# Attention stage of a fused block: transposes moved to a slot's end, projections and scores ahead of the first values

## The reference

```
x = x + 0.5 * ffn(layernorm(x))      # mixture of experts and a shared expert
x = x + attention(layernorm(x))
x = x + 0.5 * ffn(layernorm(x))

attention(X):                        # 16 query heads, 8 key/value heads, head size 32
    q, k, v = X @ Wq, X @ Wk, X @ Wv
    q, k = rope(q), rope(k)
    att = 50 * tanh(q @ k.T / 16 / 50)         # soft cap
    y = softmax(where(causal, att, -inf)) @ v
    return y @ Wo
```

## Time and profile before

| | |
|---|---|
| median of 3 runs | 1038.65 us (1037.8 to 1040.78) |
| the profiled execution | 1037.34 us, its span 1034.9 us |
| PE matmul busy | 943.6 us, 91% of the span |
| DVE, ACT, POOL busy | 631.3, 500.4, 463.0 us |
| mean granted TensorE clock | 0.981 of full |
| scores of the first slot start | 364.64 us |
| scores of the last slot start | 678.76 us |

### The profile page before, as it was taken

How to read it: one execution, slowest core, us unless ns; L and a number is a source line. 1 busy time by engine, 2 the same in 40 slices (tenths; PEclk the granted TensorE clock), 3 DMA queues, 4 the chain that set the end, 5 groups by cost and what they waited for, 6 DMA issues and landing times. The chain is left out here.

```text
span 1034.9 us, 17824 instructions
## 1 busy us (share of the span) xinstructions
PE 943.6 (91%) x6146; PEld 698.0 (67%) x6146; DVE 631.3 (61%) x1669; ACT 500.4 (48%) x733; POOL 463.0 (45%) x502
## 2 busy tenths in 40 slices
PE   2999998999999479999999999986999989999998
PEld 1788876777778446565556655544888867777787
DVE  4888777444445445656565656635888777453435
ACT  3766732132234057675667666653766532232322
POOL 5333204565541164666456645633422223655530
PEclk9999999999999699999999999998999999999999
DMA  5433235777764300000100010012243255777735
GB/s 185 117 107 113 74 102 148 173 182 179 178 152 101 123 1 21 21 20 21 41 20 21 20 41 21 12 61 75 64 130 110 69 162 124 181 184 178 177 65 167
DMA packets 95430, 101.88 MB, mean 98 GB/s; under 512 B 18688, under 2 KB 86656, under 8 KB 95360
## 3 DMA queue, kind: packets, MB, share of 16 engines
q1 hardware_dynamic: 83072, 83.17, 27.1%
q0 software_dynamic: 12288, 17.83, 10.2%
HBM read 65.44 MB, written 35.54 MB: 98 GB/s over the span
## 5 line engine op out<-in xcount | busy, mean ns | idle before, releaser
L80 PE MATMUL gu<-x_hi,gu_hi 128*128 128x512 f32 x308 | 139.1, 452 | 4.8 <-DVE act_gu L1124 4.8
L1585 POOL TENSOR_SCALAR_AFFINE_SELECT probs_at<-probs_at 128x1024 f32<-128x1024 f32 x64 | 71.1, 1111 | 133.7 <-ACT probs_at L1528 133.7
L82 PE MATMUL gu<-x_lo,gu_hi 128*128 128x512 f32 x308 | 121.9, 396 | 0.0
L81 PE MATMUL gu<-x_hi,gu_lo 128*128 128x512 f32 x308 | 121.3, 394 | 0.0
L1520 ACT ACTIVATE capped_at<-scores_at 128x2048 f32<-128x2048 f32 x64 | 93.2, 1456 | 36.8 <-PE scores_at L1434 36.8
L671 POOL DMA_INDIRECT rows<-z_rows,slots x64 | 68.8, 1075 | 75.4 <-DVE slots L1115 56.4
L957 ACT CAST a_hi<-act_gu 128x512 fp32r<-128x512 f32 x96 | 59.2, 616 | 83.8 <-DVE act_gu L1124 64.0
L1528 ACT ACTIVATE probs_at<-capped_at 128x2048 f32<-128x2048 f32 x64 | 95.0, 1485 | 2.0
L80 PE MATMUL down<-down_hi,a_hi 128*128 128x256 f32 x300 | 93.7, 312 | 0.2 <-DVE a_lo L1134 0.2
L867 PE MATMUL zT<-w_gu,xT 128*128 128x352 f32 x256 | 86.3, 460 | 0.0
L81 PE MATMUL down<-down_hi,a_lo 128*128 128x256 f32 x300 | 83.7, 279 | 0.0
(11 more groups left out here) (218 smaller groups left out, 2394.7 us busy)
## 6 DMA issues: line engine op xcount, KB each, us to landing
w_gu<-in_w_gate SPq DMA_DIRECT2D x64, 176.0 KB
w_gu<-in_w_up SPq DMA_DIRECT2D x64, 176.0 KB
w_down<-in_w_down SPq DMA_DIRECT2D x64, 176.0 KB
z_rows<-z SPq DMA_DIRECT2D x16, 512.0 KB, 3.1
acc<-base SPq DMA_DIRECT2D x10, 512.0 KB, 3.6
out<-base SPq DMA_DIRECT2D x10, 512.0 KB, 3.7
x_f<-in_X SPq DMA_DIRECT2D x8, 512.0 KB, 4.7
xn_at<-acc SPq DMA_DIRECT2D x16, 256.0 KB, 2.7
```

Of the source, the lines that this page charges most:

```text
L80: nc.tensor.matmul(out, w_hi, x_hi, start=first, stop=False)
L81: nc.tensor.matmul(out, w_lo, x_hi, start=False, stop=False)
L82: return nc.tensor.matmul(out, w_hi, x_lo, start=False, stop=last)
L1585: pool.affine_select(out=diag, in_=diag, compare_op=ALU.is_ge, fill=zero, base=0, pattern=[[0, JH], [0, REP], [1, P]], channel_multiplier= ...
```

## The change

Nothing is added or removed; instructions of the attention slots change places on PE, ACT, POOL and DVE. SP's queue is the same.

```diff
@@ TensorE
-            def slot_of(b, q, behind=True, ahead=True):
+            def slot_of(b, q, behind=True, ahead=True, further=True):
                 score_unit(b, q, 0)
-                if ahead:
-                    transposes(b + 1)
                 if behind:
                     weighted_values(b - 1, 1 - q, 3)
                 if ahead:
@@
                 score_unit(b, q, 1)
                 if ahead:
                     project(b + 1, 1 - q, 1)
+                    project(b + 1, 1 - q, 2)
+                score_unit(b, q, 2)
                 weighted_values(b, q, 0)
-                score_unit(b, q, 2)
-                if ahead:
-                    project(b + 1, 1 - q, 2)
                 weighted_values(b, q, 1)
                 score_unit(b, q, 3)
                 if behind:
                     output(b - 1)
                 if ahead:
                     project(b + 1, 1 - q, 3)
+                if further:
+                    transposes(b + 2)
                 weighted_values(b, q, 2)
@@ ScalarE
-                if ahead:
-                    aT_hi_part(b + 1)
                 cap(b, 0)
@@
                 if ahead:
                     copy_v(b + 1, 1 - q)
+                if further:
+                    aT_hi_part(b + 2)
@@ GpSimd
                 causal(b, 0)
+                if ahead:
+                    rope(b + 1, 1 - q, 0)
                 causal(b, 1)
                 if ahead:
-                    rope(b + 1, 1 - q, 0)
                     rope(b + 1, 1 - q, 1)
                 if further:
                     root(b + 2)
-                causal(b, 2)
                 if ahead:
                     rope(b + 1, 1 - q, 2)
+                causal(b, 2)
                 causal(b, 3)
@@ VectorE
+                if behind:
+                    invert(b - 1, 1)
                 if ahead:
-                    aT_lo_part(b + 1)
                     turn(b + 1, 0)
                 if behind:
-                    invert(b - 1, 1)
                     divide(b - 1, 1)
@@
                 if further:
                     normalise(b + 2)
                 invert(b, 0)
+                divide(b, 0)
                 if behind:
                     residual(b - 1)
-                divide(b, 0)
+                if further:
+                    aT_lo_part(b + 2)
```

More of the change, by code:

```diff
@@ L1493, in _ @@
                 project(0, 0, n)
+            transposes(1)
             slot_of(0, 0, behind=False)
@@ L1498, in _ @@
             slot_of(SEQS - 3, 1)
-            slot_of(SEQS - 2, 0)
-            slot_of(SEQS - 1, 1, ahead=False)
+            slot_of(SEQS - 2, 0, further=False)
+            slot_of(SEQS - 1, 1, ahead=False, further=False)
             weighted_values(SEQS - 1, 1, 3)
@@ L1555, in _ @@
             copy_v(0, 0)
+            aT_hi_part(1)
             slot_of(0, 0, behind=False)
@@ L1698, in _ @@
                 turn(0, n)
+            aT_lo_part(1)
             for b in range(SEQS):
```

## The result

The change makes the kernel slower: 1075.47 us median of 4 runs (1071.5 to 1076.49) against 1039.07 before, a ratio of 1.034 (95% interval 1.031 to 1.037). The prediction was 1068, its range 1047 to 1078. The profiled execution took 1071.5 us with a span of 1069.0; it is the fastest of the four, so what follows explains 34 of the 36 us.

A forecast was written before the change was run, and what follows sets the result against it. PE nearly bounds the kernel, with a loop from first scores through root, normalise and invert to last values almost as long. 16.1 - 2.5 + 15.5 = +29 on the median 1038.65 gives 1068 us, range 1047 to 1078.

The forecast's parts named there:

- The loop: First scores, tanh, exp, masks and ropes, root, normalise, invert, last values: almost no slack, so what the change adds costs.
- The meetings of DVE and POOL: Division beside a POOL instruction takes 1.30 us, not 0.68; first rope 0.46 late; normalise keeps DVE 2.6 us.
- The wait: PE before the moved transposes waits 2.3 us for DVE's residual; slot 22.14 us, +16.1 us over slots 1 to 13.
- The clock: PE's clock falls to half after the 2.3 us: 10 falls in 13 slots at 1.55 us each, +15.5 us.
- The ends: Slot 14, without transposes and normalising, 1.6 us less; slot 0 0.9 us less; together -2.5 us.
- A clock that stays full: PE waits before the transposes as forecast, but without the clock falling, or up to three falls: 1052 to 1057 us; chance 0.29.
- The rival of a smaller wait: DVE's divisions meet POOL at no cost, transposes start at 18.9 us, slot +0.47 us: 1042 us; chance 0.07.
- the faster case: DVE's normalising takes 0.73 us for 2.6, so PE alone bounds a slot at 19.9 us: 1023 us; chance 0.08.

The follow-up runs named there:

- residual before the division: The changed kernel with one pair swapped on DVE, the residual one place earlier, ahead of divide; 1041.1 us, ratio 1.001 to the kernel before.
- residual before invert: The changed kernel with the residual two places earlier on DVE, directly behind normalise; 1021.6 us, ratio 0.983 to the kernel before.
- root one rope earlier: The changed kernel with root on POOL moved ahead of one rope, directly behind the second mask; 1027.0 us, ratio 0.988 to the kernel before.
- division from PSUM: The changed kernel with the division reading its first operand from PSUM tile pv, not its SBUF copy; 1060.1 us, ratio 1.020 to the kernel before.
- the wait filled: The changed kernel with three more matmuls a slot on PE ahead of the transposes' wait, results unread; 1051.5 us, ratio 1.011 to the kernel before.

## Why the prediction was right, point by point

**The loop.** That almost no slack was left in scores, tanh, exp, masks, ropes, root, normalise, invert and last values carried the whole argument. Its times after the first scores, forecast and measured (528.19 taken from the rows above): root ends 13.70 and 13.64; DVE starts invert 16.34 and 16.32; division ends 18.98 and 18.95; residual ends 19.55 and 19.54; transposes start 19.70 and 19.69. The chain is shown, not only argued: the residual before the division brought the transposes forward by 0.92 us, with 0.78 for the division's link. The residual before invert ended 2.56 us earlier, with 2.55 for invert and division. The root one rope earlier ended 2.6 us earlier and the transposes started 2.1 earlier, since the division then waited for the output.

**The meetings of DVE and POOL.** Normalise 2.64 us up to invert for 2.6, the first division 1.24 for 1.3, the first `by_sin` 0.45 us longer for 0.46. The Trainium skill (SBUF — State Buffer, section on SBUF's two separate sides) has the rule that explains which instructions meet, one with two SBUF inputs, and the division from PSUM agrees with it. Its exclusive lock for the whole instruction would have made the rope 0.68 us late; the row of before, 0.46, was the better price. What the forecast left out is that the late mask also holds PE, 0.28 us a slot; the long wait covered that.

**The wait.** 2.3 forecast, 2.48 measured. PE was ready at 17.21 and not 17.4: its own work is about 0.5 shorter, of which the two projections in a row are 0.22, and the second mask takes 0.28 of that back. A full-clock slot of 22.14 was forecast, and with the wait filled it is 22.10.

**The clock.** This is the mis-sized term. I took 10 falls in 13 slots at 1.55 us, 15.5 us in all. There were 12: slots 1 to 13 took 307.2 us, and 13 x 22.10 of that is the slot at full clock, which leaves 19.9, 1.66 for each fall. (The kernel before had 0.8 of this kind too, in its slot 1, so the growth is 15.6 + 19.9 - 0.8 = 34.7.) The 10 was a choice and not a working, and that it came close was in part luck: a wait of 2.19 us brought 7 falls, one of 2.48 brought 12. That the clock would fall at 2.3 us was read from two long waits of the kernel before, and filling the wait shows that it is the cause and not a companion. The page on the clock (the Trainium skill, TensorE: Matmul & The Clock Gate, section on HAM oscillation) has a loop that pays in every round, and here it nearly did, after 12 waits of 13; in two experiments it was 10 and 7 of 13.

**The ends.** The -2.5 us forecast were -1.5 for slot 0, +0.6 for the transposes ahead of it and -1.6 for slot 14. Measured were -1.2, +1.1 and -1.5, together -1.6. Slot 14 hit its difference by two misses: it took 19.0 us where 19.3 was worked out, and the one of before took 20.5 where I had taken 20.9. For the 1.0 us behind the last slot I had nothing. Of the 7.5 us by which 1068 is short, 3.1 lie in slots 1 to 13 and 1.9 in these ends. The rest is that the changed kernel's profiled execution took 4.0 us less than its median, that of before 1.7 less.

**Rivals.** A clock that stays full would have given 1052 to 1057; the kernel with the wait filled took 1051.5, so that rival was priced within a microsecond and did not happen. The rival of a smaller wait had the meetings with POOL cost nothing, and its price of 1042 was wrong: the division from PSUM is that kernel, and it took 1060.1, since PE still waited 2.19 us and the clock fell 7 times. That residual before division took 1041.1 is chance. And the faster case, 1023, is what residual before invert gives, 1021.6, by another way than the one named: not normalise was short, but fewer links stood behind it.

## What to carry to other kernels

Moving a step ahead also moves what it waits for into the loop: list the links from the loop's start to the release, and put the releasing instruction as early in its engine's queue as its own input allows. Here two places in DVE's order were worth 54 us (1075.5 against 1021.6), far more than the move itself. Differences of a few microseconds are better read from the slots than from the whole time, since the parts outside them varied by 3 and by 5 us. A wait of PE that recurs is to be priced twice, once in time and once in the clock behind it; if it can't be removed, harmless matmuls in it can win back the second part, as they did here with 24 us.

## What the runs showed of the hardware that was not expected

- **Falls of the clock come in step with the loop.** In the changed kernel 13 falls follow each other at 23.9 us from the end of slot 0 to that of slot 12, and the slots that they lengthen take 23.7. So each comes 0.1 to 0.3 us later against its wait than the one before: the first begins 0.4 us before the transposes start, the thirteenth 1.5 us after. Behind the next wait there is none. In slots 1 to 13 the clock was lowered for 44.4 us with a wait of 2.83 us, for 41.0 with 2.48, for 23.9 with 2.19 and never with 1.57. Two waits of 2.83 and 2.81 us in one execution, and one of 2.49 at the end of the changed kernel's slots, show that the length of a wait alone does not decide. Why the one falls and the other doesn't stays open here.
- **The loss grows faster than the wait.** From 1.57 us of wait to 2.48 the time rises by 34 us, of which the wait itself explains 12 (13 x 0.9). The kernel with a wait of 2.19 us, 1060.1, lies between.
- **A meeting costs both sides.** DVE's division and POOL's next instruction each lost about 0.5 us, though the two never touch the same data. DVE's rows alone don't show why its chain was late; POOL's do.
